# One VectorE operation for the low half of a hidden block, one calculation of scales for two quads, and a later schedule of routing, in a fused GNN layer and top-2 mixture of experts on one core

## The reference

```python
x = x + gnn(LN(x))           # gnn(v): h = LN(v)*gamma + beta; agg = adj @ h
                             #         v + relu(agg @ W_rel + b_rel + h @ W_root)
x = x + ffn(LN(x))           # ffn(v): the 2 best of 8 experts for each row, softmax over the 2 scores,
                             #   each expert: relu(v @ W1[e].T + b1[e]) @ W2[e].T + b2[e], hidden size 512
```

## Time and profile before

| | |
|---|---|
| three runs | 481.05, 480.88, 479.68 us; median 480.88 us |
| profiled execution | 481.32 us, of which the span in the trace is 479.5 us |
| busy share of the span | PE 82%, DVE 66%, ACT 57%, POOL 52% |
| main loop: first to last `output` | 88.81 to 441.81 us |
| granted TensorE clock, mean | 0.936 of full speed |

### The profile page before, as it was taken

How to read it: one execution, slowest core, us unless ns; L and a number is a source line. 1 busy time by engine, 2 the same in 40 slices (tenths; PEclk the granted TensorE clock), 3 DMA queues, 4 the chain that set the end, 5 groups by cost and what they waited for, 6 DMA issues and landing times.

```text
span 479.5 us, 13216 instructions
## 1 busy us (share of the span) xinstructions
PE 393.0 (82%) x4371; PEld 350.2 (73%) x4371; DVE 315.6 (66%) x1055; ACT 271.5 (57%) x572; POOL 249.9 (52%) x263
## 2 busy tenths in 40 slices
PE   2888878789998679889867999999999999999000
PEld 2873735579997568889856988889999999998000
DVE  4875764685679497756898557765478545588511
ACT  1787583557885547786634686555555555554000
POOL 3002720177710377774007777777777750777770
PEclk9998785999999799999999999999999999999755
DMA  8991740164234234633436537647567857554520
GB/s 274 389 413 69 277 98 12 40 149 112 74 83 100 68 98 109 155 94 80 66 79 172 138 102 139 142 112 162 145 153 178 202 133 121 135 156 140 175 71 33
DMA packets 100721, 65.30 MB, mean 136 GB/s; under 512 B 66866, under 2 KB 92466, under 8 KB 100020
## 3 DMA queue, kind: packets, MB, share of 16 engines
q1 hardware_dynamic: 66292, 34.68, 27.4%
q0 software_dynamic: 8192, 16.79, 12.2%
q10 hardware_dynamic: 26176, 12.98, 11.1%
HBM read 19.58 MB, written 31.85 MB: 107 GB/s over the span
## 4 chain that ended last, share of the span: by engine, by line
PE 57%; DVE 22%; ACT 7%; issue 6%; DMA 3%; POOL 3%; ACTq 0%; SPq 0%; DVEq 0%; POOLq 0%
PE PY L951 7%; PE PY L946 7%; PE PY L947 7%; PE PH L927 6%; PE PH L929 6%; PE PH L928 6%; DVE HL L521 5%; POOL YG L307 3%; PE PY L938 2%; DVE STI L361 2%; PE PB L848 2%; PE PA L856 2%; PE PA L857 2%; ACT N L670 2%; DVE STO L407 1%
## 5 line engine op out<-in xcount | busy, mean ns | idle before, releaser
L294 POOL DMA_INDIRECT rows<-XHL,IDX x128 | 124.2, 970 | 136.0 <-DVE IDX L503 97.9
L521 DVE SCALAR_TENSOR_TENSOR HL<-PH,HH 128x512 f16<-128x512 f32 x198 | 129.9, 689 | 63.6 <-ACT HH L727 61.0
L307 POOL DMA_INDIRECT YG<-yrows,IDX x128 | 121.5, 949 | 81.7 <-DMA yrows<-YB 43.6
L727 ACT ACTIVATE HH<-PH 128x512 f16<-128x512 f32 x198 | 115.4, 594 | 29.4 <-PE PH L929 24.1
L947 PE MATMUL PY<-W2H,HL 128*128 x792 | 131.8, 220 | 0.0
L946 PE MATMUL PY<-W2H,HH 128*128 x792 | 131.8, 220 | 0.0
L927 PE MATMUL PH<-XT,W1H 128*128 128x256 f16 x396 | 108.1, 273 | 2.7 <-DVE HL L521 1.7
L951 PE MATMUL PY<-W2L,HH 128*128 x792 | 109.5, 220 | 0.0
L929 PE MATMUL PH<-XT,W1L 128*128 128x256 f16 x396 | 108.0, 273 | 0.0
L928 PE MATMUL PH<-XT,W1H 128*128 128x256 f16 x396 | 107.9, 273 | 0.0
L735 ACT ACTIVATE YB<-PY 128x256 f32<-128x256 f32 x99 | 37.9, 383 | 97.4 <-PE PY L951 92.3
(11 more groups left out here) (192 smaller groups left out, 504.8 us busy)
## 6 DMA issues: line engine op xcount, KB each, us to landing
yrows<-YB ACTq DMA_DIRECT2D x47, 256.0 KB
rows<-XT SPq DMA_DIRECT2D x2, 3072.0 KB, 16.3
YG<-in_w SPq DMA_DIRECT2D x2, 2048.0 KB, 11.3
out<-X SPq DMA_DIRECT2D x16, 256.0 KB
X<-in_x SPq DMA_DIRECT2D x3, 1024.0 KB, 5.5
ADJ<-in_adj SPq DMA_DIRECT2D x32, 64.0 KB
rows<-XHL,IDX POOLq DMA_INDIRECT x128
YG<-yrows,IDX POOLq DMA_INDIRECT x128, 2.5
```

Source lines behind the costliest of these rows:

```text
L294: nc.gpsimd.indirect_dma_start(rows[g % 2], bass.IndirectOffsetOnAxis(ap=IDX[:, col:col + 1], axis=0), XHL[:, src:src + 2 * P].bitcast(F32 ...
L307: nc.gpsimd.indirect_dma_start(YG[g % 2][:, dst:dst + P], None, yrows[g], bass.IndirectOffsetOnAxis(ap=IDX[:, col:col + 1], axis=0)).then_ ...
L521: nc.vector.scalar_tensor_tensor(HL[:, at:at + 2 * BW], PH[p % 2 * 2 + h][:, :], 0.0, HH[:, at:at + 2 * BW], ALU.max, ALU.subtract).then_i ...
L727: nc.scalar.activation(HH[:, at:at + 2 * BW], PH[p % 2 * 2 + h][:, :], ACT.Relu).then_inc((hia_made, hib_made)[h], 1)
```

## The change

Four things change, all in the main loop.

1. The two banks of a block become one PSUM tensor of 1024 fp32 numbers, and `low_halves(p)` makes the whole low half in one operation, when both high halves are there. One semaphore `lo_made` takes the place of two.
2. The scales of an even quad and of the odd one after it are calculated together, in the same 18 operations on eight numbers for four, when the odd quad's statistics are there.
3. A new table `FINISH` gives the block at which a quad is normalised, transposed and scored. It was START + 5 for every quad. It is now, in pairs, START of the odd quad + 5 and + 6: quads 6 to 15 finish at blocks 12, 13, 16, 17, 25, 26, 31, 32, 48, 49 (before: 10, 12, 14, 16, 22, 25, 28, 31, 44, 48).
4. `ROUTE` is 18, 33 and 50 for groups 2, 3 and 4 (before: 16, 32 and 49).

```diff
+FINISH = {n: START[n | 1] + 5 + n % 2 for n in START}
-ROUTE = {2: 16, 3: 32, 4: 49}
+ROUTE = {2: 18, 3: 33, 4: 50}
...
-        PH = [pb(f"PH{k}") for k in range(4)]
+        PH2 = [ctx.enter_context(nc.psum_tensor(f"PH{k}", [P, 1024], F32)) for k in range(2)]
+        PH = [PH2[k // 2][:, k % 2 * 512:k % 2 * 512 + 512] for k in range(4)]
...
-            def low_half(p, h):
-                dve.wait_ge((hia_made, hib_made)[h], p + 1)
-                at = (p % 2 * 2 + h) * 2 * BW
-                nc.vector.scalar_tensor_tensor(HL[:, at:at + 2 * BW], PH[p % 2 * 2 + h][:, :], 0.0, HH[:, at:at + 2 * BW],
-                                               ALU.max, ALU.subtract).then_inc((loa_made, lob_made)[h], 1)
+            def low_halves(p):
+                dve.wait_ge(hia_made, p + 1)
+                dve.wait_ge(hib_made, p + 1)
+                at = p % 2 * 4 * BW
+                nc.vector.scalar_tensor_tensor(HL[:, at:at + 4 * BW], PH2[p % 2][:, :], 0.0, HH[:, at:at + 4 * BW],
+                                               ALU.max, ALU.subtract).then_inc(lo_made, 1)
...
-                    if p == at + 3:
-                        scales_out_first(n, 1)
-                    if p == at + 4:
-                        scales_out_last(n, 1)
-                low_half(p, 0)
-                low_half(p, 1)
+                for n, at in FINISH.items():
+                    if p == at - 2 and n % 2 == 0:
+                        scales_out_first(n, 2)
+                    if p == at - 1 and n % 2 == 0:
+                        scales_out_last(n, 2)
+                low_halves(p)
                 for n, at in START.items():
                     if p == at + 2:
-                        stats_out(n, 0)
-                    if p == at + 5:
+                        stats_out(n, n % 2)
+                    if p == FINISH[n]:
                         split_low(n)
                         scores(n)
...
-                    if p == at + 5:
+                    if p == FINISH[n]:
                         split_high(n)
-                    if p == at + 4:
+                    if p == FINISH[n] - 1:
                         norm_out(n)
...
-                    if p >= 2:
-                        pe.wait_ge((loa_made, lob_made)[h], p - 1)
+                    if p >= 2 and h == 0:
+                        pe.wait_ge(lo_made, p - 1)
...
             def output(p, e):
-                pe.wait_ge(loa_made, p + 1)
-                pe.wait_ge(lob_made, p + 1)
+                pe.wait_ge(lo_made, p + 1)
```

More of the change, by code:

```diff
@@ L168, in build @@
         ha_done, hb_done = sem("ha_done"), sem("hb_done")
-        hia_made, hib_made, loa_made, lob_made = sem("hia_made"), sem("hib_made"), sem("loa_made"), sem("lob_made")
+        hia_made, hib_made, lo_made = sem("hia_made"), sem("hib_made"), sem("lo_made")
         y_done, y_made = sem("y_done"), sem("y_made")
```

## The result

The changed kernel takes 484.76 us (median of four runs, 483.13 to 485.44) beside 480.61 us for the kernel before (479.68 to 481.05): a ratio of 1.0084, with a 95% interval of 1.0054 to 1.0114. It is 4 us slower where I forecast +1.4 us, and its median lies 0.2 us above the range. The profiled execution is the fastest of the four, 483.13 us, of which the span is 481.3 us.

A forecast was written before the change was run, and what follows sets the result against it. PE, busy 82%, was taken to bound the kernel, its waits mostly on DVE in blocks 1 to 53. Terms +0.3 + 0.5 - 2.4 + 1.2 + 0.4 + 0.3 + 1.1 = +1.4 on 480.88 gave 482.3 us, range 478.2 to 484.6.

The forecast's parts named there:

- The price of the operation: DVE's low half of 128x1024 in every block: 1.22 us, between bounds of 1.15 and 1.35 us.
- The lateness of the low half: Low half 0.56 us later, hidden in quiet blocks: +1.1 us behind eight combines, +0.3 in blocks 0 to 4.
- group 4's rank: Blocks 39 to 54: low halves end 0.55 us later with DVE in line; 2.1 us before, 2.4 after, +0.3.
- Blocks 0 to 12: Low half's delay in blocks 0 to 4, where PE waits for DVE: +0.3 us; block 12 costs nothing.
- Blocks 13 to 19: Scales, ACT's added normalisation at block 16 and group 2's later rank: 11.9 us before, 12.4 after, +0.5.
- blocks 20 to 30: Fewer scales between low halves save 4.5 us, PE's wait at block 25 costs 2.1: -2.4 us.
- ACT's order at block 25: Odd quad's normalisation queued behind the split and next quad's h0 on ACT: PE waits 2.1 us.
- Blocks 31 to 38: Statistics and slots together in block 35, PE waiting 3.0 us at block 36: 7.4 us before, 8.6 after, +1.2.
- Blocks 39 to 54: Quads 14 and 15, pair scales at block 46 and normalisation at 48, +0.4 us; group 4's rank, +0.3.
- The clock: Rival: PE's clock holds through the 4.0 us idle stretch, 1.8 us less lost; median 480.5 us, chance 0.20.
- The relief: Rival: DVE's relief reaches further, pairs' normalisation doesn't hold PE up; -3.0 us, median 477.9, chance 0.20.
- The double operation: Rival: the merged low half takes 1.35 us, 0.13 later at 17 places; +2.2 us, median 484.5, chance 0.18.

The follow-up runs named there:

- e5: The kernel before with only the low half changed, to one 128x1024 operation: 484.9 us beside 481.5, ratio 1.0073.
- e12: e11 with the single low-half operation back in all 99 blocks: 478.0 us, ratio 0.9935.
- e11: The changed kernel with two low-half operations, scales ahead of the residual, and input statistics of groups 3 and 4 at blocks 6 and 25: 474.51 us, ratio 0.9864.
- e9: The changed kernel with the two low-half operations of before in blocks 55 to 98, the single one in blocks 0 to 54: 483.14 us, ratio 1.0036.
- e10: The changed kernel with the two low-half operations of before in blocks 0 to 54, the single one in blocks 55 to 98: 482.85 us, ratio 1.0021.
- e6: The changed kernel with the low half in two operations as before: 481.62 us, ratio 1.0001.
- e8: The kernel before with each of the two low-half operations waiting for both high halves: 487.86 us, ratio 1.0134.
- e13: The changed kernel with only the input statistics of groups 3 and 4 moved, to blocks 6 and 25: 477.71 us, ratio 0.9906.
- e14: The kernel before with only the input statistics of groups 3 and 4 moved, to blocks 6 and 25: 481.39 us, ratio 0.9999.
- e7: The changed kernel with unused matmuls added in PE's waits ahead of the three falls of the clock: 483.9 us, ratio 1.0061.

## Why the prediction was wrong

**The price of the operation** (1.22 us) was right: 1226 ns. The Trainium skill (VectorE: DVE Perf Modes, the TRN2 errata) has two formulas: (120 + elements) / 0.96 GHz for a PSUM source gives 1.19 us, which the trace does not bear out; (elements + 151) / 0.96 GHz, stated there for an fp32 addition, gives 1.224 us and 691 ns for the two sizes, and the rows say 1226 and 689.

**The lateness of the low half** was the right mechanism with too small a sum. Step that failed: I charged it +1.1 us behind the combines and +0.3 in blocks 0 to 4, with a share in the +0.3 of group 4's rank, 1.7 us at most, and by itself it costs 3.4 us (e5; 3.5 by e12 less e11). The combines measured +1.4 in the trace, and 1.6 to 2.3 us by e9. Up to block 54 e10 takes back 1.9 to 3.0 us. The periods of the changed kernel less those of e6, which differ in this alone, have it at blocks 4, 19, 29, 46 and 51: 0.3, 0.7, 0.4, 0.4 and 0.6 us. In e6 too PE is idle there, ahead of `output` or of a rank's matmul on the mask. The mask comes 0.6 us later as well (waits of 2.69 for 2.08 us at block 19, 1.27 for 0.72 at block 51), as it is made behind a low half. I added 0.56 us only at the first blocks and walked through the others with the schedule's gains in the same sum, where low half alone (+3.4) and schedule alone (0.0) should each have had one. A slip of the other sign: the 0.13 us behind a combine is reckoned from the floor, though in its own example the period before was already 0.07 us above it.

**Blocks 0 to 12**: +0.3 became +1.4. Of this 1.65 is the clock at block 2, of which the next blocks give a part back (e9, without the fall, has 7.9 for 8.7 in this stretch). I had counted no fall there, as it had not fallen behind the like wait in the trace before. No version of the low half goes with it: it is low there in the profiles of e5, e6, e8, e10, e12 and e13, and not in those of e9, e11 and e14. Another 0.9 (with smaller gains beside it) is block 11: I had the pair's scales ahead of `residual(8)` in DVE's row; in the code they stand behind it, and the residual waits until 132.71 for ACT. In e11, with the order swapped, block 11 is back at its old 0.6.

**Blocks 13 to 19**: +0.5 became +2.4. PE's waits were 4.04 (I said 4.0) and 2.54 (I said 1.9); block 16 took 7.99 us (I said 7.5); and the rank's wait was 2.69 (I said 2.6), with a stumble of 0.4. The list was right and each size was low. Blocks 14 and 16 are alike in e6 (a wait of 2.67 us, a period of 8.0), so there it is the schedule that I mis-sized; only block 19 holds lateness. With the clock up at block 16 (e7) the period is 6.2 us: the 1.8 us that I put on the clock there is right.

**Right**: blocks 20 to 30 to 0.1 us, with no wait left at 20, 23 and 26, and ACT's order at block 25, 2.1 us (L867 waited 1.83 us there). Blocks 31 to 38, +1.1 for +1.2: statistics and slots in one block, PE waiting 2.42 us at block 36 (I said 3.0). In e6 and e7, with the clock up at block 37, the 2.0 us that I had put at block 38 are there; in the changed kernel's profile they stand at block 37, at the low clock.

**Blocks 39 to 54** were -0.3 for +0.7: excesses of 0.3, 0.6 and 1.0 us at blocks 42, 43 and 50 went, and 0.4, 0.6 and 1.4 us came at blocks 46, 48 and 51, with 0.6 less at 52 and 53.

**The rivals.** The clock did not stay up, it fell twice more. I had set 3.6 us without a fall against 4.48 us with one; it fell behind waits of 2.66 and 2.42 us, so the length of the wait does not decide it. The relief did not reach further: the waits on ACT's row that I gave as the reason against it are all there. The double operation did not cost more. So +4 us is none of my three rivals. It is my own mechanism, mis-sized, with falls of the clock beside it, on the side where the range was short by 0.2 us.

**What stays open**: why e8 loses 3.3 us more than e5, which its periods show as many small pieces; and how much of the 4 us the clock makes. Within one kernel some executions are longer as the clock is lower: the changed kernel's four go from 483.13 us at a mean granted clock of 0.931 to 485.44 at 0.924, and e6's from 480.28 at 0.933 to 483.01 at 0.926, but e5's six show no such order. No run separates the lateness from the falls that a longer wait may bring on.

## What to carry to other kernels

Merging two operations that are released one after the other trades work for lateness: here DVE is busy for 8.5 us less over 99 blocks, for a result 0.6 us later in each, and it costs 3.4 us, since the engine was waited for and not full. Sum such an edit by itself: over every wait for the operation, over every wait for what is made behind it in the engine's row (here the mask), and over the blocks whose slack is less than the lateness (here the combines). A schedule change that measures as nothing may still be half of a gain: ask what the room it makes could hold (pairing with its later finish alone 0, early statistics alone 0; both, with the swap of scales and residual, 6.6 us).

## What the runs showed of the hardware

The granted clock fell to 1.2 GHz behind a wait of 2.66 us in the changed kernel, and not behind a wait of 2.67 us, with the same instructions around it, in e9. In the same way it fell behind 2.70 us at the mask of group 2 in e7, and not behind 2.69 us in the changed kernel. The Trainium skill (TensorE: Matmul & The Clock Gate, Part 1) calls the number of slow matmuls run-variable, for the phase at a kernel's start; these runs show the like in the middle of one. So one profiled execution neither shows nor excludes such a fall, and its price, 1.65 us at the period and about 0.9 net of what the next blocks gave back, belongs in the range.

A PE at half clock cost less than its busy time says: with the clock kept up in e7, block 37 lost 1.4 us of its excess and block 38 gained 1.4, as DVE's scales set the end.
